# Normalised tiles transposed by DMAs of SyncE instead of identity matmuls, in a transformer layer on eight cores

## The reference

```python
def proj(W):                       # Wq, Wk, Wv: 16 heads of 64
    return einsum('btm,nm->btn', x, W) ...
O = _flash_attention(Q, K, V, 128, 1/sqrt(64))    # causal
attn = einsum('btm,nm->btn', O, Wo)
h = silu(x1 @ w_gate.T / 127) * (x1 @ w_up.T / 127)   # 3072 wide, int weights
ffn = h @ w_down.T / 127
x1 = _layernorm(x + attn)
out = _layernorm(x1 + ffn)
```

## Time and profile before

| | us |
|---|---|
| median of 3 runs | 1301.59 |
| lowest, highest of them | 1300.77, 1461.5 |
| the profiled execution's own time | 1303.55 |
| its span, slowest core (7) | 1302.5 |
| spans of the 8 cores | 1296.7 to 1302.5 |
| granted clock of the 8 cores | 0.994 to 0.999 |

### The profile page before, as it was taken

One profiled execution on the slowest core, in us unless ns is written; L12 is line 12 of the kernel. 1 busy time (PEld: TensorE's weight loads), 2 busy tenths in 40 slices (PEclk: granted clock), 3 DMA queues, 4 the chain that ended last, 5 costly groups with the idle time before them and its releaser, 6 DMA issues.

```text
span 1302.5 us, 26270 instructions; the slowest of 8 cores (1296.7 to 1302.5 us)
## 1 busy us (share of the span) xinstructions
PE 1249.0 (96%) x9974; PEld 677.4 (52%) x9974; DVE 451.9 (35%) x813; ACT 705.1 (54%) x794; POOL 182.7 (14%) x258
## 2 busy tenths in 40 slices
PE   4989999999999999999988999999999999999997
PEld 2645656656656566665554544444444444444443
DVE  1444344343543434423344575212221322132123
ACT  0058878888788898889979755111112211301123
POOL 2001111122021120212223011210011011101100
PEclk9989999999999999999999999999999999999999
DMA  9932323224232232232745023850245134504512
GB/s 139 164 67 50 58 50 59 42 58 75 43 67 42 50 67 42 50 59 50 147 114 155 9 74 115 292 159 17 81 149 157 67 113 146 167 27 134 157 50 113
DMA packets 39448, 119.84 MB, mean 92 GB/s; under 512 B 13344, under 2 KB 13344, under 8 KB 37152
## 3 DMA queue, kind: packets, MB, share of 16 engines
q0 software_dynamic: 24672, 100.68, 32.7%
q1 hardware_dynamic: 14656, 17.47, 4.2%
HBM read 145.13 MB, written 27.39 MB: 132 GB/s over the span
## 4 chain that ended last, share of the span: by engine, by line
PE 86%; ACT 5%; another core or an unknown queue 5%; issue 2%; DVE 1%; DMA 1%; POOL 0%; SPq 0%; DVEq 0%; ACTq 0%
PE pp L357 20%; PE ops L714 16%; PE dps L1175 13%; PE gps L1121 13%; PE ups L1115 13%; PE sps L660 9%; ACT pt L670 5%; PE dps L1020 2%; DMA ident<-identd 1%; PE tps L1046 0%; DVE vbuf L400 0%; DVE pt L690 0%; ACT x1T L1052 0%; PE pp L432 0%
## 5 line engine op out<-in xcount | busy, mean ns | idle before, releaser
L670 ACT ACTIVATE pt<-sps,cbias 128x1024 bf16<-128x1024 f32 x544 | 569.9, 1116 | 89.9 <-PE sps L660 84.5
L714 PE MATMUL ops<-pt,vbuf 64*65 64x512 bf16 (+3 forms) x2560 | 328.6, 344 | 7.2 <-DVE pt L690 3.7
L1127 ACT ACTIVATE sgb<-gps 128x512 bf16<-128x512 f32 x96 | 57.3, 597 | 369.6 <-PE gps L1121 369.6
L660 PE MATMUL sps<-qbuf,kbuf 64*128 64x512 bf16 (+3 forms) x1280 | 220.5, 346 | 8.3 <-ACT pt L670 7.0
L714 PEld LDWEIGHTS ops<-pt,vbuf 64*65 64x65 bf16 x2560 | 152.9, 107 | 87.9 <-issue 25.6
L357 PE MATMUL pp<-xb,wkq 64*128 64x512 bf16 x1344 | 190.9, 380 | 2.3 <-DVE cbias L472 1.0
L1115 PE MATMUL ups<-x1T,wgu 128*128 128x512 bf16 x768 | 181.4, 379 | 0.0
L1121 PE MATMUL gps<-x1T,wgu 128*128 128x512 bf16 x768 | 181.4, 379 | 0.0
L1175 PE MATMUL dps<-wd,hbuf 128*128 128x512 bf16 x768 | 166.4, 379 | 0.0
L1130 DVE SCALAR_TENSOR_TENSOR hbuf<-ups,sgb 128x512 bf16<-128x512 f32 x96 | 66.4, 692 | 260.7 <-ACT sgb L1127 260.7
L756 POOL TENSOR_TENSOR ofm<-ostg,lb 64x512 bf16<-64x512 f32 x64 | 82.2, 1285 | 369.9 <-DMA lb<-linvd 367.5
(11 more groups left out here) (71 smaller groups left out, 606.0 us busy)
## 6 DMA issues: line engine op xcount, KB each, us to landing
wgu<-wgub POOLq DMA_DIRECT2D x96, 512.0 KB, 3.8
wgub<-wguP POOLq DMA_DIRECT2D x24, 512.0 KB, 6.0
xb<-xP POOLq DMA_DIRECT2D x8, 1024.0 KB, 36.0
lb<-linvd SPq DMA_DIRECT2D x32, 256.0 KB, 3.6
x<-xtok POOLq DMA_DIRECT2D x16, 512.0 KB, 7.5
yout<-x SPq DMA_DIRECT2D x15, 512.0 KB, 2.7
wdb<-wdP POOLq DMA_DIRECT2D x12, 512.0 KB, 6.0
wd<-wdb POOLq DMA_DIRECT2D x6, 1024.0 KB, 8.0
```

Source lines behind the costliest of these rows:

```text
L660: mm = pe.matmul(buf[:, h * 512 + so:h * 512 + so + w], kt[r, kb * 128:kb * 128 + 128], qt[r, g * 512 + q0:g * 512 + q0 + w], start=True, ...
L670: exp_at[j] = s_act.inc(act.activation(pt[j % NPT][:, :], buf[:, :], AF.Exp, bias=cbias[(p + s["late"]) % 2][:, 0:1]))
L714: mm = pe.matmul(ops[:, h * 512 + q0:h * 512 + q0 + w], vt[r, c0:c0 + 65], pt[j % NPT][r, h * 512 + so:h * 512 + so + w], start=(s["first" ...
L1127: gps_free[0] = s_act.inc(act.activation(sgb[j][:, :], gps[:, :], AF.Silu, scale=QS))
```

## The change

A tile is no longer transposed by PE. `turn(t, ready)` issues 8 transposing DMAs from SP, one for each block of 128 x 128 bf16 (32 KB), from `ybf[t % 3]` straight to `x1T`, after SP has waited for the tile and for PE to have come to `ready` (the old contents of the memory are then dead). Who writes `ybf[t % 3]` again waits for these DMAs (semaphores `s_tr[t % 3]`). In attention `turn` is due at tick +6, after `ybf_early`; `early_turn` is gone, and with it its LAST. After attention `turn(t)` follows the normalising of tile t. `gate_up(g)` waits for the DMAs of its four tiles. The bank `tps` becomes `gps[1]`, and block hc writes `gps[hc % 2]`.

```diff
         def ybf_early(t):
...
-            wait(dve, s_pe, ybf_free[t % 3])
+            wait(dve, s_tr[t % 3], ybf_free[t % 3])
...
                     pending.append((tick[0] + 5, lambda: ybf_early(t)))
+                    pending.append((tick[0] + 6, lambda n=s_pe.n: turn(t, n)))
...
-        def early_turn(t):
+        def turn(t, ready):
             g, k = t // 4, t % 4
...
+            wait(sp_q, ybf_at[t][0], ybf_at[t][1])
+            wait(sp_q, s_pe, ready)
             for c in range(NCH):
...
+                s_tr[t % 3].inc(sp_q.dma_start_transpose(
+                    x1T[g][:, c * 512 + k * 128:c * 512 + k * 128 + 128],
+                    ybf[t % 3][:, c * 128:(c + 1) * 128]), 16)
+            ybf_free[t % 3] = s_tr[t % 3].n
+            x1T_at.setdefault(g, []).append((s_tr[t % 3], s_tr[t % 3].n))
...
-                while turned[0] <= t - 2 and not over[0]:
...
-        gps = st.enter_context(nc.psum_tensor("gps", [128, 512], F32))
-        tps = st.enter_context(nc.psum_tensor("tps", [128, 1024], BF16))
+        gps = [st.enter_context(nc.psum_tensor(f"gps{i}", [128, 512], F32)) for i in range(2)]
...
         def normalised(t):
             rstd_shift(t, ln_ready[t])
-            wait(act, s_pe, ybf_free[t % 3])
+            wait(act, s_tr[t % 3], ybf_free[t % 3])
...
         for t in range(early_next[0], NTT):
             out_proj(t)
-            while turned[0] <= t - 2:
-                turn(turned[0])
-                turned[0] += 1
             if t < NTT - 1:
                 normalised(t)
             else:
                 rstd_early(t)
                 ybf_early(t)
+            turn(t, att_pe)
...
-            wait(pe, x1T_at[g][0], x1T_at[g][1])
+            for sem, value in x1T_at[g]:
+                wait(pe, sem, value)
...
-                wait(pe, s_act, gps_free[0])
+                wait(pe, s_act, gps_free[j])
...
             gate_up(g)
-            while turned[0] < NTT:
-                turn(turned[0])
-                turned[0] += 1
             down(g)
```

More of the change, by code:

```diff
@@ L205, in build_program @@
         s_cv = Sem(st, nc, "s_cv")
+        s_tr = [Sem(st, nc, f"s_tr{i}") for i in range(3)]
         dve.memset(onesb[:, :], 1.0)
@@ L781, in build_program @@
         early_next = [0]
-        turned = [0]
         over = [False]
@@ L850, in early_tiles @@
                 yield from early_half(t, 1)
-                while turned[0] <= t - 2 and not over[0]:
-                    if turned[0] in ybf_at:
-                        turned[0] += 1
-                        yield from early_turn(turned[0] - 1)
-                    else:
-                        yield WAITS
             yield from turn_on(None)
@@ L986, in build_program @@
         att_act = exp_at[NJ - 1]
-        att_dve = s_dve.n
         att_ps.close()
@@ L993, in build_program @@
         ups = [st.enter_context(nc.psum_tensor(f"ups{i}", [128, 512], F32)) for i in range(2)]
-        gps = st.enter_context(nc.psum_tensor("gps", [128, 512], F32))
-        tps = st.enter_context(nc.psum_tensor("tps", [128, 1024], BF16))
+        gps = [st.enter_context(nc.psum_tensor(f"gps{i}", [128, 512], F32)) for i in range(2)]
         dps_free = [[(s_act, att_act)] * 2, [(s_act, att_act)] * 2]
-        tps_free = [(s_dve, att_dve)]
         def rstd_shift(t, ready):
@@ L1039, in normalised @@
             ybf_at[t] = (s_act, n)
[L1041 to L1053, removed]
         wgu_free = [att_pe] * NWB
@@ L1093, in build_program @@
                 ybf_early(t)
+            turn(t, att_pe)
         wo_done = s_pe.n
         wait(pool, s_pe, wo_done)
-        gps_free = [0]
+        gps_free = [0, 0]
         ups_free = [0, 0]
@@ L1118, in gate_up @@
                 s_pe.inc(mm)
-                wait(pe, s_act, gps_free[0])
+                wait(pe, s_act, gps_free[j])
                 for c in range(NCH):
-                    mm = pe.matmul(gps[:, :], wgu[i][:, c * 128:(c + 1) * 128],
+                    mm = pe.matmul(gps[j][:, :], wgu[i][:, c * 128:(c + 1) * 128],
                                    xt[:, c * 512:(c + 1) * 512],
@@ L1126, in gate_up @@
                 wait(act, s_dve, sgb_free[j])
-                gps_free[0] = s_act.inc(act.activation(sgb[j][:, :], gps[:, :], AF.Silu, scale=QS))
+                gps_free[j] = s_act.inc(act.activation(sgb[j][:, :], gps[j][:, :], AF.Silu, scale=QS))
                 wait(dve, s_pe, max(wgu_free[i], h_free[0]))
```

## The result

The changed kernel is slower: 1368.75 us in the median of 5 runs (1359.79 to 1399.61) against 1301.59 before; ratio 1.0496, 95% interval 1.0476 to 1.0516. Its profiled execution has a span of 1367.7 us on core 7, the same core as before, and 1352.5 to 1367.7 over the cores (1296.7 to 1302.5 before).

A forecast was written before the change was run, and what follows sets the result against it. PE, busy 96%, was taken to bound the kernel. Lateness in gate_up(0) of 72X - 26.5 us less PE's gain of 12.9 gives 72X - 39.4, +40 us at X = 1.1: 1340 us, range 1293 to 1390.

The forecast's parts named there:

- The end of the path: In gate_up(0): tile 12's DMAs hold DVE at tile 15, PE stops after four runs; first product at 765.5 + 72X.
- Its beginning: End of attention: DVE normalises tile 4 at about 758; from there SP has tiles 4 to 12, 72 DMAs.
- Above: Upper bound of the DMA price, 2.0 us: SP behind from tile 0, first product at 931, time +126 us.
- steps 1 to 3: PE's gain: 6.3 us of turns before gate_up(0), 4.2 of stalls, 2.4 before down(0); together 12.9 us.
- Step 2: After attention: stalls at the first late turns, 4.2 us, go; the first named is for DVE's reciprocal.
- The price X: On SP: time from one transposing DMA to the next, issue or movement, whichever is longer; taken as 1.1 us.
- after 1 us or so into the third block all further work should be as before: In gate_up(0), after PE's gap of 72X - 26.5 us: no further change expected.
- Unit 31: After attention: linvd leaves at 758 + 16X, its chain holds SP 4 us; PE's wait, some 10, lies inside the lateness.
- rival D: On SP: one transpose in flight at a time, 1.6 to 2.7 us; lcol waits behind turns; 1380 to 1480; chance 0.10.
- A: On SP, the forecast case: transposes paced by more than issue, 0.91 to 1.6 us each; 1329 to 1379; chance 0.48.
- B: On SP: transposes at the pace of their issue, 0.45 to 0.91 us, gain and wait nearly cancel; 1296 to 1328; chance 0.36.
- C: On SP: 0.45 us or less per transpose, SP nearly level with PE, three buffers suffice; 1289 to 1295; chance 0.06.

The follow-up runs named there:

- e2_plain: Changed kernel with plain DMA copies in place of the transposing DMAs, output not the reference's: 1310 us, ratio 1.0065 to the kernel before.
- e3_half: Changed kernel with only four of each tile's eight blocks transposed, gate_up reading them twice: 1309 us, ratio 1.0057 to the kernel before.
- e5_unit31: e1_one_dma with unit 31's reciprocal and scaling due at tick +3 in place of +6: 1290.39 us, ratio 0.9916 to the kernel before.
- e8_before31: Kernel before the change with only unit 31's reciprocal and scaling due at tick +3: ratio 1.0002.
- e4_five: Changed kernel with five buffers for normalised tiles in place of three: 1347 us, ratio 1.0350 to the kernel before.
- e1_one_dma: Changed kernel with one transposing DMA of 128 x 1024 per tile in place of eight: 1295 us, ratio 0.9946 to the kernel before.
- e7_beside: Kernel before the change plus 80 transposing DMAs beside gate_up(0) that only SP waits for: 1307 us, ratio 1.0041.

## Why the prediction was right, by its steps

- **The end of the path: right.** DVE held by `ybf_early(15)`, that by tile 12's DMAs, PE by `ups[0]` after four runs. By the sum, 765.5 + 72 x 1.31 = 859.8 is when the first product is done; the third block, which it releases, began at 856.05. With five buffers the sum gave 838.9 against 837.45.
- **Its beginning: right by luck.** The sum starts at 758, where tile 4 was to be normalised and SP was to be free. DVE normalised tile 4 at 742.61, and SP came to it at 757.97 because it was already late: it began tile 2 at 736.25, though DVE had normalised it from 725.72 on. The path in fact runs from tile 0, 13 tiles or 104 DMAs. The forecast has that sum under "Above", for X = 2.0; with 1.31 it gives 715.9 + 104 x 1.31 + 4 + 3.5 = 859.6, and the two sums happen to meet at this X. When a tile costs SP half as much, SP isn't late in attention and tile 4 goes out before 758, so one tile less is left than the sum has: in `e2_plain` and `e3_half` SP began tile 5 at 758.61 and 757.81, ACT's path ended last, and the third block came 4 us before the sum. That the ends agreed all the same (+8.1 against +8.5, +7.0 against +7.4) is partly luck, as the time lost after the stall makes up for it.
- **PE's gain, steps 1 to 3: right in size.** 12.9 summed, 11 realised in `e5_unit31`. Step 2 took from the trace that the reciprocal is the stall; `e8_before31` shows that it wasn't (the reciprocal earlier, the waits and the time the same). In the changed kernel that wait was replaced by a longer one, 10.11 us for DVE.
- **The price X: mis-sized, and for a wrong reason.** Taken 1.1 as a middle between issue and landing, measured 1.31: 72 x 0.21 = 15 us short in the forecast's own sum. Along the path from tile 0, with 104 DMAs, it is 22 us, of which the start at 758 had hidden 7: at 1.1 that sum gives 837.8, the forecast's 844.7. I expected movement and completion to pace it. It is SP's time for the instruction, 1.20 in the median, also for the first three in an idle queue (3.66 us), and also with eight times the data. It is no constant beside loads of weights: single ones took up to 2.43 us here, 4.85 in `e4_five` and 6.12 in `e5_unit31`. The Trainium skill's 1309 ns for a 128 x 128 block (VectorE: DVE Perf Modes, "The three transpose paths") stands beside 1.31 from issue to issue; `e1_one_dma` shows it to be a price of the instruction and not of the block. The Trainium skill's rule that transposing DMAs are as fast as plain ones (Advanced Engine Details and Errata, "X-Bar Transpose (TRN2)") fails here at 32 KB, 1.31 against 0.66.
- **A term that was missing: what comes after the stall.** On cores 0, 3, 5 and 6 the rest of `gate_up(0)` took 77 to 79 us, on cores 2 and 4 it took 81 and 84, on cores 1 and 7 it took 89 and 90, with PE waiting for gate weights. The time is that of the slowest core, so +12, of which some 3 are two runs at the lower clock after the longest wait (901.27 to 907.68, 6.4 us in place of 3.46; granted 0.55 from 901 to 908). Another 1.6 us is the clock after the pause: granted 0.61 in the mean from 803 to 856, and the first run took 3.37 us in place of 1.73 (856.05 to 859.42). Since the transposes alone make PE wait for weights (`e7_beside`), "after 1 us or so into the third block all further work should be as before" was wrong.
- **Unit 31: its time right, its size wrong.** `linvd` at 758 + 16X = 779, measured 778.84, with the same luck in the 758. But `lcol` had already waited in the queue behind transposes: DVE began to copy the unit at 748.0, and SP issued its column at 768.25. That is rival D's sign at a price of A. It cost nothing of its own, as the lateness at tile 15 took it in; and SP was held 1.7 us from `linvd` to `lb`, not 4.
- **Eight tiles projected in attention, not seven.** The half tile begun was finished. It moved work and cost nothing.
- **Rivals.** B's mechanism is real and was seen at the price of a plain DMA. C is what one DMA per tile makes of the change. D's price, 2.0, did not occur, but its condition did: SP was late in attention at 1.31. The chances of A and D add up to 0.58, not 0.57.

By the forecast's own sum, +40 became +65 by 15 us of X and 14 us of the missing term, less 4 us by which the third block came before the sum's 859.8. Of these, 2.3 are the 72 transposes themselves, which took 92.1 us or 1.28 each; 0.8 is unit 31, whose DMAs held SP 3.2 us in all, not 4; the rest is the last DMA's landing, which the sum adds behind its issue though they overlap. The time lay in the range.

## What to carry to other kernels

A DMA that replaces engine work moves the cost to the queue that issues it: count the instructions there against the time in which the producer delivers, before counting bytes. When the count is what costs, put the whole tile into one instruction: here that turned +5.0% into -0.5%, and with the small DMAs that others wait for moved ahead of it, -0.8%. The queue that fell behind didn't hurt where its result is used (`gate_up` never waited for `x1T`), but where its source buffer is written again, and in the small transfers that stood behind it. And before adding up such a queue, look whether it is already late where the sum begins.

## What the runs showed of the hardware that was not expected

- A transposing DMA took SP 1.20 to 1.22 us, whether for one block of 128 x 128 bf16 or for eight; a plain one of one block 0.60. Landing: 2.3, 3.1 and 1.9 us.
- Beside loads of weights the transposes suffered too: landing 10.6 us in the median from 856 to 905 us, and SP's time for 80 of them rose to 120.00 us in `e4_five`.
- Transposes in flight slowed plain loads very unevenly over the cores: 512 KB of weights in 7.9 us on one core and 5.1 on another of the same run, where the kernel before had 4.4 and 5.1.
